# A three-layer graph network on one core: one-hots from ScalarE to VectorE, and a third chunk of single-row fetches

## The reference

```python
def gat_conv(x, edge_index, W, att_src, att_dst, bias):
    h = (x @ W).reshape(N, HEADS, HEAD_DIM)              # 4 heads of 32
    a_src = jnp.einsum('nhc,hc->nh', h, att_src)
    a_dst = jnp.einsum('nhc,hc->nh', h, att_dst)
    e = a_src[src] + a_dst[dst]
    e = jnp.where(e > 0, e, NEG_SLOPE * e)
    e_max = jax.ops.segment_max(e, dst, num_segments=N)
    ex = jnp.exp(e - e_max[dst])
    denom = jax.ops.segment_sum(ex, dst, num_segments=N)
    alpha = ex / (denom[dst] + 1e-16)
    return jax.ops.segment_sum(h[src] * alpha[:, :, None], dst, num_segments=N).reshape(N, HIDDEN) + bias
...
x = _layernorm(x + relu(gat_conv(relu(gat_conv(x, ...)), ...)))
msgs = z[edge_dst] @ Wd + z[edge_src] @ Ws + edge_weight[:, None] * ww[None, :] + bm
agg = jax.ops.segment_max(msgs, edge_dst, num_segments=n)
hidden = jax.nn.relu(z @ W1a + agg @ W1b + b1)
x = _layernorm(x + hidden @ W2 + b2)
```

## Time and profile before

| | us |
|---|---|
| median of 3 runs | 9389.37 (9385.1 to 9401.34) |
| profiled execution | 9408.25 |
| its span, first to last instruction | 9406.5 |
| VectorE busy | 4126.2 (44%) |
| ScalarE busy | 4671.4 (50%) |
| GpSimd busy | 4892.1 (52%) |
| TensorE matmuls busy | 5335.8 (57%) |

### The profile page before, as it was taken

One profiled execution on the slowest core, in us unless ns is written; L12 is line 12 of the kernel. 1 busy time (PEld: TensorE's weight loads), 2 busy tenths in 40 slices (PEclk: granted clock), 3 DMA queues, 4 the chain that ended last, 5 costly groups with the idle time before them and its releaser, 6 DMA issues.

```text
span 9406.5 us, 142120 instructions
## 1 busy us (share of the span) xinstructions
PE 5335.8 (57%) x24591; PEld 4985.0 (53%) x24591; DVE 4126.2 (44%) x11944; ACT 4671.4 (50%) x10625; POOL 4892.1 (52%) x5157
## 2 busy tenths in 40 slices
PE   4755555555556646655555555564455555555556
PEld 4655555555556546555555555564444444444445
DVE  2533433334334614433334333355455445545457
ACT  2645555455555545545555455565344444444447
POOL 4455555555555545545555455545555555555552
PEclk6555555555555655555555555556677677766678
DMA  5222222222222322222222222225455455444555
GB/s 146 64 55 61 62 60 61 60 60 61 63 61 67 76 64 60 62 59 60 61 61 62 58 60 62 62 55 169 119 128 130 119 127 130 128 124 127 128 141 141
DMA packets 731716, 812.60 MB, mean 86 GB/s; under 512 B 176926, under 2 KB 545694, under 8 KB 730670
## 3 DMA queue, kind: packets, MB, share of 16 engines
q1 hardware_dynamic: 570110, 471.14, 18.3%
q0 software_dynamic: 158240, 331.14, 15.1%
q10 hardware_dynamic: 2448, 0.74, 0.0%
HBM read 753.64 MB, written 48.89 MB: 85 GB/s over the span
## 4 chain that ended last, share of the span: by engine, by line
SPq 29%; issue 21%; DVE 4%; PE 4%; another core or an unknown queue 4%; ACT 1%; DMA 1%; DVEq 1%; POOL 0%; ACTq 0%; POOLq 0%
SPq L454 12%; SPq L429 5%; SPq L452 2%; SPq L693 2%; SPq L691 2%; DVE acc L1668 2%; PE bS L1006 1%; PE bA L953 1%; SPq L544 1%; SPq L569 1%; DVE bA L1916 1%; SPq L545 1%; DVE ch L1922 1%; DMA st<-d_neg 0%
## 5 line engine op out<-in xcount | busy, mean ns | idle before, releaser
L839 POOL DMA_INDIRECT G<-table,idx x3286 | 3108.7, 946 | 2964.7 <-PE bS L1006 1134.8
L1006 PE MATMUL bS<-G,S 128*128 x8816 | 2171.8, 412 | 929.7 <-issue 356.3
L953 PEld LDWEIGHTS bA<-adst,st 128*128 128x128 f32 x7872 | 1803.2, 332 | 1238.4 <-ACT st L1261 992.6
L1006 PEld LDWEIGHTS bS<-G,S 128*128 128x128 f32 x8816 | 1873.9, 299 | 1057.8 <-issue 806.9
L953 PE MATMUL bA<-adst,st 128*128 x7872 | 1706.3, 340 | 1197.0 <-ACT st L1261 973.4
L1277 ACT ACTIVATE S<-iota_row,nd 128x128 f32<-128x128 f32 x5904 | 1869.0, 388 | 647.8 <-issue 503.2
L839 POOL DMA_INDIRECT G<-ztable,idx x1643 | 1554.2, 946 | 1170.0 <-issue 438.6
L1256 ACT ACTIVATE st<-xd,neg_p 128x512 f32<-128x512 bf16 x972 | 690.5, 710 | 2535.3 <-DMA xd<-d_drel 2000.6
L1668 DVE TENSOR_TENSOR acc<-acc,bS 128x136 f32 (+1 forms) x4408 | 1277.9, 290 | 589.3 <-remote 286.7
L1281 ACT ACTIVATE S<-S,one_col 128x512 f32<-128x512 f32 x1476 | 1065.9, 722 | 50.3 <-ACT S L1277 2.3
L1664 DVE SCALAR_TENSOR_TENSOR acc<-bS,acc 128x132 f32 x610 | 179.2, 294 | 1400.6 <-PE bS L1006 779.9
(11 more groups left out here) (223 smaller groups left out, 4017.3 us busy)
## 6 DMA issues: line engine op xcount, KB each, us to landing
xd<-d_drel SPq DMA_DIRECT2D x328, 384.0 KB
xd<-in_ew SPq DMA_DIRECT2D x312, 256.0 KB
st<-d_neg SPq DMA_DIRECT2D x312, 256.0 KB
wide<-table SPq DMA_DIRECT2D x4608, 0.5 KB
G<-table,idx POOLq DMA_INDIRECT x3286
isend<-in_ew SPq DMA_DIRECT2D x104, 256.0 KB
isend<-d_neg SPq DMA_DIRECT2D x104, 256.0 KB
G<-ztable,idx POOLq DMA_INDIRECT x1643
```

The source lines that it names most:

```text
L839: pool.indirect_dma_start(G[:, r, c, 0:width], None, from_table, bass.IndirectOffsetOnAxis(ap=idx[:, r, c:c + 1], axis=0)).then_inc(gather ...
L953: mm = pe.matmul(bA[:, bass.ds(chunks[s], HEADS)], st[:, i % 3, s, :], adf[:, bass.ds(tiles[s], HEADS)], start=False, stop=True, skip_grou ...
L1006: mm = pe.matmul(bank_of(l, u, r, k)[:, j * w:(j + 1) * w], S[:, onehots(r, i), s, :], chunk_at[0][s], start=True, stop=True)
```

## The change

- VectorE makes the one-hots of the 52 batches, in all three layers: one comparison a quad (`hot_quad`), 128 x 512, of `iota_row` with four columns of `nd`. It does so three quads ahead (`HOT`), right after it has added quad i up. `iota_row` now holds 0, -1, ..., -127. ScalarE still makes the 24 quads of the tails.
- `WIDE_R` = (3, 4, 2): three chunks in five batches are fetched by rows. `WIDE_BY` gives r = 3 to SyncE and r = 4 and 2 to ScalarE, in all three layers. `WIDE_STEPS` spreads them: SyncE's chunk at 32 rows in each of the four batches ahead of its use; ScalarE's at 55, 55 and 18 rows in the three batches ahead, and at 37, 55 and 36 in the batches four, three and two ahead. Of five bodies ScalarE has 36 rows in one and 55 in four, SyncE 32 in four and none in one.
- ScalarE's body in a graph layer is now nine times: distance, hits, a ninth of its rows (at most seven); after the fifth pair the exponents. In the max layer it is eight times: copy back, an eighth of its rows.
- The numbers of the rows are uint16 in place of int32.

```diff
-WIDE_R = (3, 1)
+HOT = 3
+WIDE_R = (3, 4, 2)
+WIDE_BY = (ENG.SP, ENG.Activation, ENG.Activation)
+WIDE_EVEN = ((4, 0, 32), (3, 32, 64), (2, 64, 96), (1, 96, P))
+WIDE_EARLY = ((3, 0, 55), (2, 55, 110), (1, 110, P))
+WIDE_LATE = ((4, 0, 37), (3, 37, 92), (2, 92, P))
+WIDE_STEPS = (WIDE_EVEN, WIDE_EARLY, WIDE_LATE)
...
     def select_pair(l, u, r, it, k):
...
-                    pe.wait_ge(s_made, quad(l, u, i) + 1)
+                    if ahead:
+                        pe.wait_ge(s_made, made_by_act(l, UQ * (u - NB) + i))
+                    else:
+                        pe.wait_ge(s_hot, made_by_dve(l, u, i))
...
+            def wide_rows(l, k, it, lo, hi):          # ScalarE
+                to, width = (table[l], TW) if l < 2 else (ztable, HID)
+                sem_in, _ = wide_landed(l, WIDE_R[k], it)
+                if lo == 0:
+                    act.wait_ge(*wide_listed(l, k, it))
+                    act.nop(nofuse=True)
+                    if wide_free(l, WIDE_R[k], it) is not None:
+                        act.wait_ge(*wide_free(l, WIDE_R[k], it))
+                        act.nop(nofuse=True)
+                rows = [to[bass.ds(at, 1), :] for at in registers(regs_wide[0:1, k, lo:hi])]
+                for row in rows:
+                    act.lower_ap_dma(row)
+                for j, row in enumerate(rows):
+                    act.dma_start(wide[lo + j:lo + j + 1, k, 0:width], row).then_inc(sem_in, 16)
...
                 def body(b, r, it):                    # ScalarE, graph layers
-                    old(4)
-                    expand(0, 1)
-                    old(5)
...
+                    for i in range(UQ):
+                        if i < x_quads:
                             distance(l, b + 4, xr_, xit, i)
                             hits(l, b + 4, xr_, xit, i)
+                        if i == 4:
+                            weights(b, r)
+                        wide_part(l, r, it, i, UQ)
...
+            def hot_quad(l, u, r, it, i):              # VectorE
+                nodes = nd[:, r, i * QS:(i + 1) * QS].unsqueeze(2).to_broadcast([P, QS, P])
+                vec.tensor_tensor(S[:, onehots(r, i), :, :], iota_row[:, :].unsqueeze(1).to_broadcast([P, QS, P]), nodes, ALU.is_equal).then_inc(s_hot, 1)
+
+            def edge_quad(l, u, r, it, i):
+                select_quad(l, u, r, it, i)
+                if i + HOT < UQ:
+                    hot_quad(l, u, r, it, i + HOT)
+                elif not isinstance(u, int) or u + 1 < NB:
+                    hot_quad(l, u + 1, (r + 1) % RING, it + (r + 1) // RING, i + HOT - UQ)
```

More of the change, by code:

```diff
@@ L454, in wide_rows @@
                         sp.dma_start(wide[p + j:p + j + 1, k, 0:width], row).then_inc(sem_in, 16)
[L456 to L462, removed]
-            def wide_part(l, b, r, it, j, parts):
[L465 to L473, removed]
-                        continue
[L475 to L481, removed]
+            def wide_part(l, b, r, it, j, parts):
+                for k in range(NW):
+                    if WIDE_BY[k] != ENG.SP:
+                        continue
+                    for at, lo, hi in wide_steps(k, r, it):
+                        first, last = lo + (hi - lo) * j // parts, lo + (hi - lo) * (j + 1) // parts
+                        if last > first:
+                            wide_rows(l, k, at, first, last)
+                    at = wide_list_due(k, r, it)
+                    if j == parts - 1 and at is not None:
+                        sp.dma_start(regs_wide[0:1, k, :], d_wide[bass.ds(RING * at + WIDE_R[k], 1), :]).then_inc(wide_idx, 16)
             def idx_load(l, b, r, it):
@@ L1218, in scalar_program, with registers, wide_rows, wide_part @@
             act.dma_start(c_first[:, :], first).then_inc(in_first, 16)
+            def registers(v):
+                _, values = nc.values_load_multi_w_load_instructions(
+                    v, engines=[ENG.Activation], min_val=0, max_val=N_NODES - 1, bass_reorder=False,
+                    skip_runtime_bounds_check_because="the source of an edge is a node")
+                return values
+            def wide_rows(l, k, it, lo, hi):
+                to, width = (table[l], TW) if l < 2 else (ztable, HID)
+                sem_in, _ = wide_landed(l, WIDE_R[k], it)
+                if lo == 0:
+                    act.wait_ge(*wide_listed(l, k, it))
+                    act.nop(nofuse=True)
+                    if wide_free(l, WIDE_R[k], it) is not None:
+                        act.wait_ge(*wide_free(l, WIDE_R[k], it))
[5 more added lines that the diff above has]
+                    act.dma_start(wide[lo + j:lo + j + 1, k, 0:width], row).then_inc(sem_in, 16)
+            def wide_part(l, r, it, j, parts):
+                for k in range(NW):
+                    if WIDE_BY[k] != ENG.Activation:
+                        continue
+                    for at, lo, hi in wide_steps(k, r, it):
+                        first, last = lo + (hi - lo) * j // parts, lo + (hi - lo) * (j + 1) // parts
+                        if last > first:
+                            wide_rows(l, k, at, first, last)
+                    at = wide_list_due(k, r, it)
+                    if j == parts - 1 and at is not None:
+                        act.dma_start(regs_wide[0:1, k, :], d_wide[bass.ds(RING * at + WIDE_R[k], 1), :]).then_inc(wide_idx_act, 16)
             def attention(l, frm):
@@ L1273, in select_quad @@
                     act.nop(nofuse=True)
[L1274 to L1275 removed]
+                act.wait_ge(sel_done, 2 * (quad(l, u, i) - 4))
                 for s in range(QS):
[L1277 to L1279 removed]
+                    step = act.activation(S[:, onehots(r, i), s, :], iota_row[:, :], ACT.Abs, scale=-1.0, bias=nd[:, r, i * QS + s:i * QS + s + 1])
+                step.then_inc(s_made, 1)
+                act.wait_ge(s_made, made_by_act(l, n) - 1)
                 flat = S[:, onehots(r, i), :, :].rearrange("p s f -> p (s f)")
@@ L1438, in body @@
                     for s in range(NS):
-                        if some and s < 2:
-                            select_quad(l, b - 1, pr, pit, 7 + s)
                         if s >= 1:
-                            select_quad(l, b, r, it, s - 1)
                             rows(b, r, s - 1)
```

151 lines of the change are left out of this document (63 added, 88 removed).

## The result

The change makes the kernel faster: 8,997.24 us (8,978.8 to 9,019.0, four runs) against 9,387.24, a ratio of 0.9583 (0.9556 to 0.961), 390 us less, where the sum had 137. The profiled execution took 9,009.4 us (span 9,007.6) against 9,408.

The account below looks back on a forecast made before the run. SyncE's queue, full of row fetches, was taken as the bound. Terms of -162, +15, +20 and -10 gave -137 us, so 9,250 us (-1.5%) was predicted from 9,389.4, with 8,800 to 9,680 at 8 in 10.

Parts of the forecast that it names:

- The bound moves from SyncE to ScalarE: Graph layers: SyncE's queue at 292 us per five batches stops binding, needing 177; ScalarE binds at 283.
- 18 x (283 - 292): Main term: nine laps of five batches in each of two graph layers, from 292 to 283 us each: -162 us.
- the price of a row on ScalarE: ScalarE's queue, graph layers: 0.85 us per fetched row, 256 rows a lap; called the weakest step.
- this alone gains nothing: Taking one-hots off ScalarE frees 90 us a lap, already covered by its 116 us of waiting, so no gain.
- its lower price: Lower end for a row on ScalarE: 0.67 us, including 0.484 us for a register load of four, from the max layer.
- VectorE's +15 us in batches without rows: The 14 graph batches without row fetches: comparisons on the serial path cost 0 to +48 us, taken as +15.
- -10 for the copies: Third copy into G costs 0.23 us a lap, one gather fewer gives back more: -10 us over 27 laps.
- The +20 in the max layer: Max layer: VectorE's comparisons, largely covered by its waits for mask rows, cost 0 to +60 us, taken as +20.
- Rival A: ScalarE has slack at 0.67 us a row: graph lap falls to 248 us, time about 8,620; chance 0.17.
- Rival B: ScalarE's queue saturates in graph layers, a row costing over 0.887 us; at 0.95, about 9,700 us; chance 0.26.
- Rival C: VectorE's SBUF comparisons and GpSimd's gathers hold each other up: +18 us a lap, about 9,740 us; chance 0.04.
- Rival D: The bound moves but nothing comes of it: ScalarE at 290 to 293 us, time about 9,390; chance 0.09.

Follow-up runs that it names:

- e7: The changed kernel with ScalarE's two row-fetched chunks and none on SyncE; 1.0588 of the kernel before, on a chip where that takes 6,741 us.
- e8: The changed kernel with two chunks by rows, one on SyncE and one on ScalarE; 1.0217 of the kernel before, which takes 6,741 us there.
- e12: The changed kernel with int32 row numbers in place of uint16; 6,960.75 us, 1.0319 of the kernel before, which takes 6,741 us there.
- e3: The changed kernel with int32 row numbers in place of uint16; 9,099 us, 0.9453 of the kernel before, which takes 9,623 us there.
- e4: The changed kernel with no chunk fetched by rows, GpSimd gathering all; 8,881 us, 0.9213 of the kernel before, which takes 9,623 us there.
- e13: The kernel before, unchanged, as base on a held-up chip; 9,410 us.
- e15: The kernel before with only the one-hots of the 52 batches moved to VectorE; 0.9627 of the kernel before, which takes 9,410 us there.
- e6: The whole change, unaltered, on a quick chip; 1.0598 of the kernel before, which takes 6,741 us there.
- e17: The kernel before with one-hots on VectorE, plus five idle ScalarE activations after each graph-layer expansion; 1.0183 of the kernel before, which takes 6,754 us there.
- e5: The kernel before, unchanged, as base on a quick chip; 6,741 us.
- e11: The changed kernel with no chunk fetched by rows, on a quick chip; 1.0295 of the kernel before, which takes 6,741 us there.

## Why the prediction was right and wrong

*The bound moves from SyncE to ScalarE:* that it leaves SyncE is right; ScalarE's vanished wait for xd and SyncE's new waits show it. That ScalarE's queue then bounds is shown by intervention on quick chips (e7, e8 and e12). On held-up chips the chain speaks for it (28%), but the runs don't prove it: in seven laps 212 us of ScalarE's idle time end with an unknown queue and 61 with TensorE, and on the chip of e3 and e4 taking every row away, 206 us a lap of ScalarE's queue, shortened the graph lap by 4.6 us only. So another bound stands close beneath, which the prediction did not have; what it is stays open.

*The size:* wrong, -390 instead of -137; 8,997 us is under the forecast's own 9,020 to 9,470, though inside the 8,800 to 9,680 given 8 chances in 10. The sum went by 18 x (283 - 292); measured are 18 x (266.8 - 292.0) = -454. Two steps failed. The first is the price of a row on ScalarE, 0.85 us, taken because a full queue had paid 0.9: it was 0.811 (10 us a lap), and ScalarE's other terms were 59 for 65 (6 us). The second is "this alone gains nothing", said of the one-hots. It counted only ScalarE's idle time, and took SyncE's 0.9 as given. The runs show that with the one-hots on VectorE SyncE's row falls from 0.867 to 0.806 us (e13, e15) and the kernel's time by 3.7%. The prediction had said itself that the price isn't constant, and then held it constant through a change of what the engines issue. It also had no term for the two-byte numbers: its lower price took the loads of four at 0.484 us, which in the changed kernel take 1.06 or more. That e6 comes to the predicted 0.67 us a row all the same is luck: issue and address cost 0.42 there where 0.55 had been read, the load 0.25 where 0.12 had.

*Moving the rows:* the sum gave the whole gain to this. On top of the one-hots it is worth 0.4% (0.9585 against 0.9627 on one chip; the intervals 0.9562 to 0.9609 and 0.9603 to 0.9652 just meet). Without them it costs 3.1%.

*The small terms:* VectorE's +15 us in batches without rows and -10 for the copies: the graph layers give 43 us less than 18 laps alone would, and the stages between 17, together 60 lost where 5 were put. The last four batches take 50.8 us each instead of 49.5. The +20 in the max layer: -5 measured, so VectorE's waits for masks covered the comparisons, the largest row falling from 245 us to 175. SyncE's loads of four numbers there went from a median of 0.495 to 1.044 us with uint16, which had no term in the sum.

*Rival A* (lap at 248): not reached; with no rows at all e4 has 264.5, on a chip 2.5% slower, so the 247.5 us of the last four batches were too low a floor. e4's own last four take 49.8 us each, 249 a lap.

*Rival B* (ScalarE saturates): its place and mechanism are what happens on quick chips, at a point that the prediction had not drawn. It decides where ScalarE's queue stands over what bound the kernel before. On quick chips it has 172 + 47 = 219 us against GpSimd's 197, at a row price of 0.67 that the prediction had counted as ScalarE's slack; on held-up chips ScalarE's lap is 267 against SyncE's 292.

*Rival C* (the port): I gave it nothing on the ground that line 1724 and the gathers are not stretched in the kernel before. The new comparison does stretch gathers, but only those that begin while it runs: in the changed kernel 1.14 us in the mean with 0.2 to 0.4 us of it left, 1.36 with 0.4 to 0.6, at most 1.47. A gather that began first takes at most 0.955, and the comparison beside one takes 686 ns in the mean, 684 alone. The kernel before showed it already: of its ten gathers that begin while line 1724 runs, four take 1.06 to 1.07 us, and 1,069 ns is the longest gather of its graph layers. The mean of 946 hid them. The Trainium skill, page "SBUF — State Buffer", section "Who interferes with whom", had the pair right, and these traces agree, in one direction only. The price is 158 x 0.026 to 0.044 = 4 to 7 us of GpSimd's time a lap, which is on the path where GpSimd binds: about 4 of the 4.7 us by which e17's lap is longer than e5's. On held-up chips its share of the lap isn't shown. The +18 us a lap of the rival were too much.

*Rival D:* no; the time moved far beyond 0.2%.

**Left open.** What holds up the queues on two of the five chips and in the first result, and why moving the one-hots changes it; whether ScalarE's instruction count or the pace of the one-hots does that; what sets a graph lap of 264.5 us on a held-up chip when no rows are fetched; whether one chunk on each engine is better than the change there. No version here beats the kernel before on a quick chip (the nearest is e17's 1.018, with its idle work); on a held-up chip the one without row fetches (e4, 0.9213) beats both.

## What to carry to other kernels

A queue's price per instruction is not a property of the queue. Where single instructions of 29 ns sometimes take over a microsecond, ask what the change does to the hold-ups before you multiply a count by the old price, and count every engine that issues. When work is moved from a full queue to another, add up the receiving queue against the next bound, not against the old one: three chunks by rows were one too many where the queues ran freely, and where they were held up the kernel with none was the fastest. And when two parts of a change rest on one bound, price each alone: here one part gave nearly all, and the other alone lost.

## What the runs showed of the hardware

The same kernel takes 6,741 us on one chip and 9,410 on another, at the same granted clock in the graph layers (0.50), with gathers of 945 and 943 ns and equal medians of the MOVEs and DMA issues of the row fetches (29 and 228 ns). (In the max layer the granted clock differs too, 0.83 against 0.69, so its laps are no clean comparison.) The difference in the graph layers goes with hold-ups in single register instructions and DMA issues of SyncE, ScalarE and TensorE, up to 1.4 us in a row fetch. On the one kind of chip a MOVE takes 29 ns without gathers and 456 in the mean with seven in 8 us; on the other it takes 29 ns at the same density. They come without any row fetches too (e4: 202 of 750 register instructions of SyncE over 0.3 us, 178 of 2,565 of TensorE; e11: none). A change tuned on one kind of chip had the opposite sign on the other: 0.9585 and 1.06.

A gather that begins on GpSimd while a VectorE comparison of 128x512 with both inputs in SBUF runs takes up to 1.47 us instead of 0.95, the longer the more of the comparison is left. A gather that began first is not stretched (at most 0.955 us in the changed kernel), and neither is the comparison.

Loading four registers from two-byte numbers takes 1.06 to 1.16 us, from four-byte ones 0.48 to 0.59; for six the two cost about the same, 1.47 and 1.51 (medians of e6 and e12).
